# Padded routing matmuls, a static list of table loads and a new order of steps in a two-layer decoder kernel

## The chip, the cores and the metric

The kernel runs on one core of one Trainium2 chip. Its time is device microseconds; "before" is the median of 3 runs. The engines are PE (TensorE, with its weight loads as PEld), DVE (VectorE), ACT (ScalarE), POOL (GpSimd) and SP, which issues most DMAs.

## The reference

The input is x, 2 batches of 512 tokens with 128 features, fp32. Six sublayers follow one another, each as

```
x = layernorm(x + f(x))
```

with these f, in order:

1. a Hawk block: RMS norm, `z = xn @ W_in.T`, a causal convolution of 4 taps on one half, gates `sigmoid(xc @ W_gates.T + b)`, a linear recurrence `h = alpha*h + beta*inp*xc`, `gelu(gate)*h @ W_out.T`, and a gated MLP;
2. cross-attention with 8 heads to a context of 32 positions, masked;
3. causal attention with 16 heads from 32-wide latents with rotary parts, then 1 shared and 7 routed experts, the 2 best with weights `scores / sum(scores)`;
4. a selective state-space recurrence with 16 states per feature, `h = exp(delta*A)*h + delta*x*B`, `y = sum(h*C)`;
5. cross-attention with 4 heads that scales and shifts a diagonal state-space convolution (done as a discrete Fourier transform by matmuls), and an MLP of width 512;
6. two shared experts (together 352 wide, padded to 3 units of 128) and 8 routed experts of width 176 (11 units of 128), the 2 best.

Routing picks by rank; the weight of each routed expert is per token:

```
wts = sum(one_hot(idx, ER) * scores[..., None], axis=1)
combined = einsum('tei,eih,te->th', silu(g) * u, Wd_r, wts)
```

## The kernel before, in words

Features (or tokens, for scores and routing) lie on the 128 partitions, and an operation mostly handles a tile of 128 x 512, one batch's tokens. The batches are two lanes, a and b, each with a 16-slot workspace (`AR`), 4 of the 8 PSUM banks (`own(b, i)`) and its own list of steps per engine (`STEPS`). A third lane, w, holds work on weights alone (`STEPS_W`): folded projections of both cross-attentions, centred weights, the tables of the state-space kernel (`dt`, `z`, `a`, `dc` on 128 x 128 tiles, then `tP` to `Q` on POOL, `s1` to `eQ` on ACT, `r1.` to `P` on DVE, `kp` on PE), in two halves 0 and 1.

Each step is a piece of a Python generator that ends in `yield`: waits on semaphores of other steps (`after`), one or some instructions, and a count on its own semaphore (`done`). `take_turns` merges the three lanes of an engine into one in-order queue by the hand-held list `TURNS`: "a4 w1" is four steps of a, then one of w. An instruction behind a waiting one on its engine waits too. SP has an order of its own: loads, then a's drafts and stacks for attention (`parts(0)`), a wait for both batches' `xa.o`, two loads, `parts(1)`.

Steps that the prediction names, in a lane's order. Hawk block: `h1.sq`, norm, `z0` to `z3`, convolution (`cv` on ACT, `cw` on DVE), four gate steps `g0` to `g3` of two 128-deep fp32 matmuls each (two PE passes per matmul), tanh `tf`, `ti`, then `al`, `sa`, `lb`, `hb` on ACT, scans `h0`, `h1` on DVE, output matmul `rg` (line 553), norm `h4`, growth `gr`, `shr`, `ln1`, which ends in DVE's `X1`. Context attention: scores `xa.s` (line 581, with the mask row added by line 582), softmax on DVE and ACT, `xa.o` (line 596), `ln2`. Latents: `lat`, `kf`, `q0`, `q1`, `v` (line 621), the rotation on DVE, the split of keys and queries into three bf16 parts (a on DVE, b on POOL). Attention: for each of 8 pairs of heads five score tiles whose row maxima DVE takes (`mx0.A` to `mx7.E`); the maxima are split, transposed (`nmt`), copied by ACT into `wT` and sent by a DMA into the query stack; then 40 score units `su` with an Exp each, values `pv` and a normalisation. Experts (`units`): for unit k a gate matmul (line 729), an up matmul (line 734), from unit `shared` on a routing matmul (line 745), which spreads the token weights of one expert over 128 partitions, and a down matmul (line 756); ACT takes a tanh of the gate, DVE multiplies three times. The scan: for each of 16 states PE spreads B and C (`bn`, `cn`, lines 803 and 797, bf16, 96 rows), ACT makes the decay (`aa`) and a copy (`bb`), POOL a product (`by`), DVE a scan (`sc`, line 1659) and a product (`hc`), PE adds it up (`yn`, line 810). In `sel0` and `sel1` the rows behind the 21 or 24 used ones are zero.

In ACT's helper `f`, a change of activation function to one that the loaded table set lacks puts a table load in the queue, behind the waits of that step and in front of its activation.

Of the kernel before, what the change touches and what calls it, by code (L numbers as in the profile page):

```python
# [19 lines left out]
BF16 = mybir.dt.bfloat16  # L20
# [8 lines left out]
J = 32  # L29
# [23 lines left out]
KROWS = MROWS + 3  # L53

# [66 lines left out]
def _centre(t):  # L121
# [54 lines left out]
    "pool": ["va0", "va1", "e1", "fb.r", "fb.s", "fb.c", "bh", "bf", "bf1", "se0", "se1", "la", *[f"dc{i}" for i in range(1, 24)], "hd.c",  # L176
# [15 lines left out]
    "dve":  # L192
# [7 lines left out]
    "act":  # L200
# [6 lines left out]
    "pool":  # L207
        "w23 b1 w1 b5 w24 a2 w3 a3 w1 a4 b1 a1 b2 a2 b1 a1 b3 a3 b1 a1 b6 w1 b3",
}

# [46 lines left out]
def build(nc, dram, out):  # L257
    lay = layouts()
    with ExitStack() as ctx:
# [176 lines left out]
        def take_turns(engine, programs):  # L436

            for turn in TURNS[engine].split():
                for _ in range(int(turn[1:])):
                    next(programs[turn[0]])  # L440
            for program in programs.values():
                assert next(program, "end") == "end", engine
# [1824 lines left out]
```

## Time and profile before

| | |
|---|---|
| median of 3 runs | 563.76 us (562.29 to 564.13) |
| the profiled execution | 561.39 us |
| its span, first to last instruction | 559.6 us |
| PE busy | 471.7 us, 84% |
| DVE busy | 355.7 us, 64% |
| ACT busy | 294.1 us, 53% |
| POOL busy | 123.0 us, 22% |
| mean granted TensorE clock | 0.928 |

The profiled execution is 1.8 us longer than its span. All durations of the rows below belong to it. A share of busy time is a mean over stages; the chain of waits is followed back from the last instruction, at each step to what released it or to the instruction before it on its engine. An fp32 matmul shows as two records, one per pass.

### The profile page before, as it was taken

To read this page: it belongs to the slowest core of one execution; us is meant where nothing else is said; L and a number is where in the kernel's file an instruction comes from. 1 tells how busy PE (TensorE), PEld (TensorE's weight loads), DVE (VectorE), ACT (ScalarE), POOL (GpSimd) and SP (SyncE) were. 2 spreads that over 40 slices of the span, in tenths; PEclk is the share of its full clock that TensorE was granted. 3 is DMA by queue.
4 is the path that set the end of the run, shared out by engine and by line. 5 is a ranking of instruction groups with operands and counts; after the bars stand their busy time and mean duration, and the time that the engine had idled before them with its cause. 6 is when DMAs were issued, how large, how long until landed. Compare 5 with 4: busy or idle time off the path is not lost.

```text
span 559.6 us, 5894 instructions
## 1 busy us (share of the span) xinstructions
PE 471.7 (84%) x2098; PEld 210.6 (38%) x2098; DVE 355.7 (64%) x619; ACT 294.1 (53%) x447; POOL 123.0 (22%) x125
## 2 busy tenths in 40 slices
PE   5949867667859989998899758789899889999995
PEld 1523322332314544443343213337646334343331
DVE  1485835546875854556888899886452264676764
ACT  4736784514104657788559866475145274542123
POOL 2000300000630008108454977334000000000000
PEclk9968796957887999999999979989999999999999
DMA  8920000633360000033000000060000000000001
GB/s 311 273 112 1 1 0 0 182 45 129 116 112 3 0 5 2 1 152 150 1 2 0 1 0 0 11 234 1 0 1 0 0 1 0 0 1 1 0 1 38
DMA packets 8983, 26.38 MB, mean 47 GB/s; under 512 B 2959, under 2 KB 6768, under 8 KB 7664
## 3 DMA queue, kind: packets, MB, share of 16 engines
q1 hardware_dynamic: 8852, 25.91, 14.8%
q8 instruction: 16, 0.26, 0.2%
q10 hardware_dynamic: 102, 0.10, 0.1%
q14 instruction: 13, 0.11, 0.1%
HBM read 21.98 MB, written 3.67 MB: 46 GB/s over the span
## 4 chain that ended last, share of the span: by engine, by line
PE 56%; DVE 17%; ACT 11%; POOL 6%; issue 5%; DMA 3%; SPq 1%; DVEq 0%; ACTq 0%
ACT AR L1012 7%; PE PS L756 5%; PE PS L729 5%; DVE AR L1339 5%; PE PS L734 5%; PE PS L818 4%; DVE stats L1348 4%; PE PS L659 3%; ACT L1011 3%; POOL RR L2024 3%; PE PS L673 3%; PE PS L527 3%; POOL AR L1936 3%; PE PS L547 2%; DMA AR<-in_s4d 2%
## 5 line engine op out<-in xcount | busy, mean ns | idle before, releaser
L1012 ACT ACTIVATE AR<-PS 128x512 f32<-128x512 f32 (+1 forms) x198 | 111.6, 594 | 118.3 <-PE PS L729 59.8
L1936 POOL TENSOR_TENSOR AR<-AR 128x512 f32<-128x512 f32 (+2 forms) x48 | 53.4, 1128 | 96.1 <-DVE AR L1339 74.4
L1012 ACT ACTIVATE AR<-AR 128x512 f32<-128x512 f32 (+2 forms) x72 | 43.8, 618 | 55.8 <-DVE AR L1339 38.0
L1011 ACT ACT_TABLE_LOAD x38 | 48.8, 1283 | 23.5 <-PE PS L527 6.1
L1339 DVE TENSOR_TENSOR AR<-PS,AR 128x512 f32<-128x512 f32 x74 | 50.3, 686 | 11.8 <-PE PS L797 3.6
L1348 DVE TENSOR_REDUCE stats<-PS 128x1 f32<-128x512 f32 (+4 forms) x88 | 43.4, 524 | 19.1 <-PE PS L645 7.6
L1345 DVE SCALAR_TENSOR_TENSOR AR<-AR,PS 128x512 f32<-128x512 f32 x44 | 29.8, 683 | 25.0 <-ACT AR L1012 24.7
L1659 DVE TENSOR_TENSOR_SCAN AR<-PS,AR 128x512 f32<-128x512 f32 x32 | 38.5, 1215 | 6.1 <-POOL AR L1936 4.3
L2024 POOL TENSOR_TENSOR RR<-KL,lags 128x512 f32<-128x512 f32 x24 | 28.2, 1211 | 62.3 <-PE PS L662 52.1
L642 PE MATMUL PS<-RR 97*128 97x512 bf16 (+3 forms) x128 | 32.6, 325 | 7.3 <-DVE stats L1348 3.6
L527 PE MATMUL PS<-AR,W_sq 128*128 128x512 f32 x44 | 25.9, 673 | 13.9 <-ACT AR L1012 13.8
L1345 DVE SCALAR_TENSOR_TENSOR AR<-PS,AR 128x512 f32<-128x512 f32 x44 | 30.1, 688 | 8.9 <-PE PS L745 4.8
L810 PE MATMUL PS<-AR,W_sq 128*128 128x512 f32 x64 | 34.3, 626 | 1.5 <-issue 1.5
L659 PE MATMUL PS<-RR 100*128 100x512 bf16 (+3 forms) x128 | 30.5, 313 | 3.8 <-DMA RR<-wT 2.2
L756 PE MATMUL PS<-AR,RR 128*128 128x512 f32 x56 | 30.8, 633 | 0.0
L729 PE MATMUL PS<-x_in,RR 128*128 128x512 f32 x56 | 28.6, 598 | 1.5 <-DVE AR L1345 1.5
L734 PE MATMUL PS<-x_in,RR 128*128 128x512 f32 x56 | 28.8, 596 | 0.0
L1012 ACT ACTIVATE AR<-PS,W_vec 128x512 f32<-128x512 f32 (+1 forms) x32 | 21.9, 696 | 12.4 <-PE PS L527 4.2
L1339 DVE TENSOR_TENSOR AR<-AR 128x512 f32<-128x512 f32 (+4 forms) x36 | 22.4, 640 | 5.8 <-ACT AR L1012 5.3
L1012 ACT ACTIVATE PS<-AR,W_vec 128x512 f32<-128x512 f32 x32 | 21.8, 689 | 7.7 <-DVE AR L1659 7.6
L797 PE MATMUL PS<-AR,select 96*128 96x512 bf16 x32 | 13.1, 415 | 10.8 <-DVE AR L1339 10.7
L673 PE MATMUL PS<-AR,Vaug 128*9 128x512 f32 (+3 forms) x256 | 21.8, 434 | 0.0
(231 smaller groups left out, 790.6 us busy)
## 6 DMA issues: line engine op xcount, KB each, us to landing
RR<-in_dft SPq DMA_DIRECT2D x1, 4096.0 KB, 12.1
RR<-in_ffn SPq DMA_DIRECT2D x1, 2688.0 KB, 9.6
RR<-in_ones SPq DMA_DIRECT2D x2, 832.0 KB
RR<-in_ones SPq DMA_DIRECT2D x2, 784.0 KB
RA<-in_moe SPq DMA_DIRECT2D x1, 1539.5 KB, 6.3
W_mla<-in_mla SPq DMA_DIRECT2D x1, 1504.0 KB, 16.8
W_late<-in_late SPq DMA_DIRECT2D x1, 1076.0 KB, 10.9
RA<-in_xa SPq DMA_DIRECT2D x1, 1056.0 KB, 8.6
```

The lines of the kernel that those rows point to most:

```text
L527: mm(own(b, i), w("sq", "ones"), A(b, 1), start=True, stop=True).then_inc(*done("pe", b, f"{t}.{step}"))
L659: mm(ring[:, c:c + n_], Kst[b][0:KROWS, h, 128 * kb:128 * kb + 128], Qst[b][0:KROWS, h, 128 * kb:T], start=(c == 0), stop=False)
L729: mm(own(b, 0), w(group, "g", 128 * k, 128), x, start=True, stop=True)\
L734: mm(own(b, 1), w(group, "u", 128 * k, 128), x, start=True, stop=True)\
L756: mm(own(b, 3), w(group, "d", 128 * j, 128), A(b, 6 + j % 2), start=(j == 0 and base is None), stop=(k == n))\
L1011: nc.scalar.preload_act_table_set(tables[loaded[0]])
L1012: nc.scalar.activation(out_, in_, func, bias=bias, scale=scale).then_inc(*done("act", *step))
L1339: nc.vector.tensor_tensor(out_, a, b_, op).then_inc(*done("dve", *step))
L1345: nc.vector.scalar_tensor_tensor(out_, a, s1, b_, op0, op1).then_inc(*done("dve", *step))
L1348: nc.vector.tensor_reduce(out_, a, X, op).then_inc(*done("dve", *step))
L1936: nc.gpsimd.tensor_tensor(out_, a, b_, op).then_inc(*done("pool", *step))
L2024: last = nc.gpsimd.tensor_tensor(out_[:, q:q + n], a[:, q:q + n], b_[:, q:q + n], op)
```

## The change

Three edits.

1. `wT` gets 96 rows instead of 48, `krowb` 96 instead of 1. Both are zeroed by POOL (steps `kz`, `wz0`, `wz1`), and the routing matmuls (line 745) and the mask-row matmuls (lines 582 and 833) read 96 rows. DVE's first write of `krowb` waits for `kz`, ACT's first write of `wT` for `wz`.
2. ACT's table loads stand in a static list `TABLES`, by place in the queue: `take_turns` calls `load_tables(n)` ahead of step n, and so ahead of its waits. The list has 30 entries.
3. `TURNS` is new for all four engines. In it b's steps of the Hawk block follow a's at a shorter distance on PE, DVE and ACT; on PE all of b's latents stand in front of a's first maximum; b's experts and b's scan come later relative to a's scan; POOL splits b's keys and queries ahead of `dc1` to `dc23`. DVE's Hawk block also waits for the load of `vec`. Of the long lists the first two lines stand below.

```diff
--- before.py
+++ after.py
@@ -51,6 +51,7 @@
 ZROWS = 49
 MROWS = PRODUCTS * HD + ZROWS
 KROWS = MROWS + 3
+WROWS = 96
 
 
 def _ln(t):
@@ -173,7 +174,7 @@
             *_centre("w2"), "hd.s", "hd.m",
             *[f"{n}{h}" for h in HALVES for n in ("r1.", "q1.", "r2.", "q2.", "rQ0.", "qQ0.", "rQ1.", "qQ1.", "P")],
             "ed.s", "ed.m"],
-    "pool": ["va0", "va1", "e1", "fb.r", "fb.s", "fb.c", "bh", "bf", "bf1", "se0", "se1", "la", *[f"dc{i}" for i in range(1, 24)], "hd.c",
+    "pool": ["kz", "va0", "va1", "e1", "fb.r", "fb.s", "fb.c", "bh", "bf", "bf1", "se0", "se1", "wz0", "wz1", "la", *[f"dc{i}" for i in range(1, 24)], "hd.c",
              *[f"{n}{h}" for h in HALVES for n in ("tP", "tQ", "aP", "aQ", "U1", "U2", "V", "Q")], "ed.c"],
 }
 
@@ -181,32 +182,39 @@
 
 TURNS = {
     "pe":
-        "a4 w1 a5 w3 a1 w1 a1 w2 a2 b1 a3 b2 a1 b2 a2 b3 a1 b1 a3 b1 a1 b1 a3 b4 a1 b7 a2 b1 a9 b4 a1 b1 a29 b1 "
-        "a2 b1 a1 b1 a2 b1 a1 b2 a2 b1 a1 b1 a1 b2 a1 b1 a3 b3 a3 b2 a1 b1 a2 b2 a3 b2 a1 b1 a2 b1 a1 b1 a1 b2 "
...
+        "a4 w1 a5 w6 a1 b1 a1 b2 a1 b2 a1 b4 a4 b1 a2 b4 a1 b1 a1 b1 a1 b1 a1 b2 a3 b2 a2 b7 a36 b1 a1 b1 a3 b3 "
+        "a1 b5 a2 b1 a1 b1 a1 b1 a1 b1 a2 b2 a1 b1 a1 b1 a1 b2 a1 b1 a1 b1 a2 b1 a1 b1 a2 b3 a2 b1 a2 b2 a1 b2 "
...
     "dve":
-        "a7 w2 a1 w3 a1 w6 a1 w1 a4 w1 a1 w3 a2 w1 a1 w6 a1 w2 a1 w3 b1 w3 b1 w2 b1 w1 b2 a1 b2 a1 w2 a6 w2 a3 "
-        "b1 a1 b5 a1 b2 a1 b2 a1 b1 a5 b2 a4 b12 a4 b1 a5 b1 w1 a1 b1 w1 b3 a34 b16 a1 b7 a1 b7 a2 b14 a1 w1 a3 "
...
+        "a2 w4 a5 w1 a2 w6 a1 w1 a1 w5 a1 w1 a3 w8 a1 w1 a1 w4 b1 w1 a1 w1 b7 a1 b1 w5 a1 b6 a1 b1 a2 b1 a2 b1 "
+        "a6 b2 a2 b2 a1 b9 a8 b1 a2 b6 a36 b1 a4 b2 a4 b9 w1 b1 w1 b12 a1 b8 a1 b6 a1 b1 a1 b4 a5 w1 b1 a1 b1 "
...
     "act":
-        "a1 w2 a2 w1 a3 w1 a1 w1 b1 w1 a17 b2 w1 b1 a1 b1 a2 b2 w2 a1 b2 a1 b3 a1 b2 a1 b3 a1 b2 a7 b2 a1 b3 a5 "
-        "b20 a1 b1 a37 b1 a4 b2 a1 b1 a1 b2 a1 b6 a1 b4 a1 b10 a1 b2 a1 b1 a1 b2 a1 b2 a1 b5 a1 b3 a1 b3 a1 b1 "
...
+        "a4 b1 w2 a3 w1 a1 w2 a1 w1 a10 b1 a1 b1 a2 b2 a1 b1 w1 a1 b1 w1 b3 w1 b9 a3 b1 a1 b2 a1 b2 a2 b1 a1 b1 "
+        "a1 b1 a6 b1 a1 b3 a4 b1 a1 b13 a31 b1 a8 b1 a1 b1 a1 b1 a1 b1 a1 b1 a2 b6 a1 b5 a1 b3 a2 b1 a1 b1 a1 "
...
     "pool":
-        "w23 b1 w1 b5 w24 a2 w3 a3 w1 a4 b1 a1 b2 a2 b1 a1 b3 a3 b1 a1 b6 w1 b3",
+        "w14 b1 w1 b5 w35 a4 w1 a3 w3 a6 w1 a4 b12 w1 b5",
 }
+
+
+
+TABLES = (
+    "1:log 8:gelu 10:log 11:exp 22:log 33:gelu 38:sin 44:log 60:gelu 62:log 182:exp 195:sin 199:exp "
+    "211:log 215:exp 219:log 221:exp 226:log 227:exp 240:sin 246:exp 263:log 346:gelu 350:log 361:gelu "
+    "370:log 373:exp 376:log 378:exp 402:log")
 
 
 def steps_of(engine, lane):
@@ -347,7 +355,7 @@
                                     sb("tmask", [128, B * NT // 4], U32))
         kmask, krow, tmask = (m[:, :].bitcast(U8) for m in (kmask_w, krow_w, tmask_w))
         tmaskf = sb("tmaskf", [128, B * NT])
-        krowb = sb("krowb", [1, B * (H0 + H1) * J], BF16)
+        krowb = sb("krowb", [WROWS, B * (H0 + H1) * J], BF16)
         pre = flat(0, 11, 14)
         kmaskf, KTs, VTs, K1s, Vrep = (pre[:, 0:512], pre[:, 512:768], pre[:, 768:1024], pre[:, 1024:1088],
                                        pre[:, 1088:1344])
@@ -364,7 +372,7 @@
         stats = sb("stats", [128, B * 1024])
         parts48 = sb("parts", [128, B, NT, 48], BF16)
         spb = [parts48[:, b] for b in range(B)]
-        wT = [sb(f"wT{b}", [48, T], BF16) for b in range(B)]
+        wT = [sb(f"wT{b}", [WROWS, T], BF16) for b in range(B)]
         Vaug = [sb(f"Vaug{b}", [128, NT, NH, HD + 1]) for b in range(B)]
         KL = sb("KL", [128, NT, 128])
         Kf = sb("Kf", [128, 2, NFB, 128])
@@ -433,11 +441,12 @@
         block = ctx.enter_context(nc.Block())
 
 
-        def take_turns(engine, programs):
-
-            for turn in TURNS[engine].split():
-                for _ in range(int(turn[1:])):
-                    next(programs[turn[0]])
+        def take_turns(engine, programs, before=lambda n: None):
+
+            lanes_ = [turn[0] for turn in TURNS[engine].split() for _ in range(int(turn[1:]))]
+            for n, lane in enumerate(lanes_):
+                before(n)
+                next(programs[lane])
             for program in programs.values():
                 assert next(program, "end") == "end", engine
 
@@ -579,7 +588,7 @@
                     for i in range(2):
                         c = own(b, p)[:, 256 * i:256 * i + 256]
                         mm(c, Xin[b][:, 128 * (2 * p + i):128 * (2 * p + i) + 128], M0[:, b, :], start=True, stop=False)
-                        last = mm(c, w("bf", "one")[0:1, :], krowb[:, 256 * b:256 * b + 256], start=False, stop=True)
+                        last = mm(c, w("bf", "one")[0:WROWS, :], krowb[:, 256 * b:256 * b + 256], start=False, stop=True)
                     last.then_inc(*done("pe", b, f"xa.s{p}"))
                     yield
                 for p in range(2):
@@ -742,7 +751,7 @@
                         elif k > shared:
                             pe.wait_ge(*after("dve", b, f"{d}w{k - 1}"))
                         if k >= shared:
-                            mm(own(b, 2), w(sel, "s", 128 * (k - shared), 128)[0:3 * e, :], wT[b][0:3 * e, :],
+                            mm(own(b, 2), w(sel, "s", 128 * (k - shared), 128)[0:WROWS, :], wT[b][:, :],
                                start=True, stop=True).then_inc(*done("pe", b, f"{p}w{k}"))
                             yield
                     if k:
@@ -830,7 +839,7 @@
                 for i in range(NT):
                     c = own(b, 2)[:, 128 * i:128 * i + 128]
                     mm(c, Xin[b][:, 128 * i:128 * i + 128], M1[:, b, :], start=True, stop=False)
-                    last = mm(c, w("bf", "one")[0:1, :], krowb[:, 512 + 128 * b:640 + 128 * b], start=False, stop=True)
+                    last = mm(c, w("bf", "one")[0:WROWS, :], krowb[:, 512 + 128 * b:640 + 128 * b], start=False, stop=True)
                 last.then_inc(*done("pe", b, "xb.s"))
                 yield
                 pe.wait_ge(*after("dve", b, "xb.p"))
@@ -1004,11 +1013,15 @@
                       "sin": "silu_and_others"}
             in_all = (ACT.Square, ACT.Copy, ACT.Identity, ACT.Abs)
             loaded = ["none"]
+            at_step = dict(x.split(":") for x in TABLES.split())
+
+            def load_tables(n):
+                if str(n) in at_step:
+                    loaded[0] = at_step[str(n)]
+                    nc.scalar.preload_act_table_set(tables[loaded[0]])
 
             def f(out_, in_, func, step, bias=0.0, scale=1.0):
-                if func not in in_all and func not in sets.get(loaded[0], ()):
-                    loaded[0] = "log" if func == ACT.Exp else next(k for k, v in sets.items() if func in v)
-                    nc.scalar.preload_act_table_set(tables[loaded[0]])
+                assert func in in_all or func in sets[loaded[0]], (step, func, loaded)
                 nc.scalar.activation(out_, in_, func, bias=bias, scale=scale).then_inc(*done("act", *step))
 
             def root(b, t, i):
@@ -1133,10 +1146,11 @@
                     act.wait_ge(*after("act", "w", "sy"))
                     act.wait_ge(*after("dve", "w", "a6"))
                     act.wait_ge(*after("pool", "w", "dc23"))
+                act.wait_ge(*after("pool", "w", f"wz{b}"))
                 act.wait_ge(*after("pe", b, "nmt"))
                 f(wT[b][0:48, :], own(b, 0).bitcast(BF16)[0:48, 0:T], ACT.Copy, (b, "nmt"))
                 act.wait_ge(*after("act", b, "nmt"))
-                act.dma_start(Qst[b][MROWS:KROWS, :, :], wT[b][:, :]).then_inc(stack["m", b], 16)
+                act.dma_start(Qst[b][MROWS:KROWS, :, :], wT[b][0:48, :]).then_inc(stack["m", b], 16)
                 yield
                 for n in range(GROUPS * UNITS + LAG):
                     if n < GROUPS * UNITS:
@@ -1330,7 +1344,7 @@
                 f(KL[:, :, :].rearrange("p j d -> p (j d)"), own(0, 0), ACT.Copy, ("w", "kl"))
                 yield
 
-            take_turns("act", {"a": batch(0), "b": batch(1), "w": shared_program()})
+            take_turns("act", {"a": batch(0), "b": batch(1), "w": shared_program()}, load_tables)
 
 
         @block.vector
@@ -1361,6 +1375,7 @@
                 tt(Xin[b][:, :], src, A(b, 7), ALU.mult, (b, name))
 
             def hawk(b):
+                dve.wait_ge(loads["vec"], 16)
                 dve.wait_ge(*after("act", b, "h1.r"))
                 stt(A(b, 2), Xin[b][:, :], vec("g1"), A(b, 7), ALU.mult, ALU.mult, (b, "xn1"))
                 yield
@@ -1790,10 +1805,11 @@
                     dve.wait_ge(loads[n], 16)
                 copy(kmaskf, kmask, ("w", "km"))
                 yield
-                copy(krowb[:, :], krow, ("w", "kb0"))
+                dve.wait_ge(*after("pool", "w", "kz"))
+                copy(krowb[0:1, :], krow, ("w", "kb0"))
                 yield
                 mine("w", "kb0")
-                ts(krowb[:, :], krowb[:, :], -1.0, BIG, ALU.add, ALU.mult, ("w", "kb1"))
+                ts(krowb[0:1, :], krowb[0:1, :], -1.0, BIG, ALU.add, ALU.mult, ("w", "kb1"))
                 yield
                 copy(tmaskf[:, :], tmask, ("w", "tm"))
                 yield
@@ -1974,6 +1990,8 @@
                     yield
 
             def shared_program():
+                nc.gpsimd.memset(krowb[:, :], 0.0).then_inc(*done("pool", "w", "kz"))
+                yield
                 for b in range(B):
                     nc.gpsimd.memset(Vaug[b][:, :, :, :], 1.0).then_inc(*done("pool", "w", f"va{b}"))
                     yield
@@ -2004,6 +2022,9 @@
                 mine("w", "se0")
                 tt(select[0:96, :], select[0:96, :], third[2], ALU.add, ("w", "se1"))
                 yield
+                for b in range(B):
+                    nc.gpsimd.memset(wT[b][:, :], 0.0).then_inc(*done("pool", "w", f"wz{b}"))
+                    yield
 
                 def quarters(table, l):
                     return table.rearrange("p (q i) l -> p q i l", q=4)
```

## Rows read from the trace of the kernel before

**Rows 1.** Stages: length, busy us (instructions) by engine, PE clock, DMA share, GB/s.
```profile
42.00:126.00 84.00, 63.44 (x139) 25.44 (x138) 45.44 (x79) 47.76 (x69) 5.97 (x11) 0.78 0.17 38
126.00:165.00 39.00, 30.36 (x132) 11.46 (x130) 31.57 (x69) 8.38 (x13) 14.22 (x19) 0.85 0.48 128
165.00:180.00 15.00, 11.26 (x73) 5.89 (x74) 6.82 (x15) 7.10 (x12) 0.00 (x0) 0.68 0.01 3
180.00:300.00 120.00, 111.62 (x808) 50.02 (x800) 82.82 (x160) 84.40 (x133) 40.24 (x34) 1.00 0.09 37
300.00:400.00 100.00, 82.63 (x440) 42.02 (x440) 80.77 (x97) 61.36 (x97) 58.67 (x45) 0.95 0.10 34
400.00:560.00 160.00, 145.60 (x403) 62.15 (x402) 87.96 (x159) 62.94 (x91) 0.00 (x0) 0.99 0.01 4
```

**Rows 2.** The chain that ended last, pieces: start us, us, what.
```profile
36.08 3.80 PE PS L553 x4
...
59.45 0.70 DVE x_in L1339
...
87.02 3.78 PE PS L553 x4
...
101.79 1.08 PE PS L621 x8
...
123.46 3.70 PE PS L596 x4
...
153.43 1.39 DVE stats L1348 x3
...
156.55 1.39 DVE stats L1348 x3
...
165.89 3.75 DMA RR<-wT
...
552.54 1.28 ACT L1011
```

**Rows 3.** PE's timeline, a unit of the tail and rows of the scan: start, us.
```profile
534.48 1.02 PE L734 MATMUL PS<-x_in,RR 128*128 128x512 f32 x2
535.44 0.39 PE L745 MATMUL PS<-wT,RR 24*128 24x512 bf16 x1
535.75 1.13 PE L756 MATMUL PS<-AR,RR 128*128 128x512 f32 x2
536.72 1.02 PE L729 MATMUL PS<-x_in,RR 128*128 128x512 f32 x2
...
341.05 0.38 PE L797 MATMUL PS<-AR,select 96*128 96x512 bf16 x1
341.26 1.02 PE L810 MATMUL PS<-AR,W_sq 128*128 128x512 f32 x2
342.12 0.38 PE L803 MATMUL PS<-AR,select 96*128 96x512 bf16 x1
```

**Rows 4.** Loads of x (SP issue, DMA landing) and POOL's first memsets.
```profile
L447 SPq DMA_DIRECT2D x_in<-in_x x2: 377/936/1494, 0.7 to 4.7; - x2
...
DMA to landing us min/median/max: 3.2/6.5/9.8
...
0.71 1.10 POOL L1978 MEMSET Vaug<- 128x576 f32 x2 [0.29 <-POOLq L2260]
```

**Rows 5.** The page's group of table loads: count, busy, mean ns, idle before.
```profile
L1011 ACT ACT_TABLE_LOAD x38 | 48.8, 1283 | 23.5 <-PE PS L527 6.1
```

**Rows 6.** ACT's timeline around the load for `dt`: start, us, idle before.
```profile
18.10 1.28 ACT L1011 ACT_TABLE_LOAD   x1 [1.75 <-DMA AR<-in_s4d]
19.39 0.31 ACT L1012 ACTIVATE AR<-AR 128x128 f32<-128x128 f32 x1
```

**Rows 7.** DVE's groups of 297 to 400 us: count, busy, mean ns, idle before.
```profile
L1659 DVE TENSOR_TENSOR_SCAN AR<-PS,AR 128x512 f32<-128x512 f32 x32 | 38.5, 1215 | 6.1 <-POOL AR L1936 4.3 <-ACT PS L1012 1.4
L1339 DVE TENSOR_TENSOR AR<-PS,AR 128x512 f32<-128x512 f32 x36 | 24.2, 683 | 4.5 <-PE PS L797 3.6
```

30 rows, old and new, of the table TURNS are left out of this document.

## The prediction

> **What bounds the kernel now.** I read the busy time by stage first, then the chain that ended last, then single rows. I call the two batches a and b; b runs about 42 us behind a. The stages [rows 1] show three regimes. Up to 126 us (Hawk block, context attention, latents of both batches) no engine is full: in 42 to 126 TensorE is busy 63.4 us of 84 although its granted clock is only 0.78, that is, it moves between 1.2 and 2.4 GHz, ACT 47.8 and DVE 45.4. This stretch is bound by latency: PE, ACT and DVE hand one 0.6 to 0.9 us operation to each other. From 126 to 165 the row maxima of batch a bound it, on DVE. From 180 on TensorE is the bound: 111.6 of 120 us, and 145.6 of 160 us from 400. Between them, 300 to 400, PE has 17.4 us idle; there DVE, with 80.8 us, carries the two recurrences (32 scans of 1.2 us [rows 7]).
>
> The chain of waits [rows 2] gives marks that I use below: a's `rg` ends at 39.9, a's `X1` is at 59.5, b's `rg` at 87.0, a's values at 101.8, b's context output matmul at 123.5 to 127.2, the maxima at 3.12 us per pair of heads, and the 3.75 us DMA of a's row maxima into the query stack at 165.9.
>
> **Part 1, padding the small matmuls to 96 rows.** The edit makes 36 routing matmuls (14 in the first expert layer, 22 in the second) and 8 mask-row matmuls read 96 rows instead of 21, 24 or 1. What it changes is read from start to start [rows 3]. In an expert of the tail: up projection at 534.48, routing matmul (24 rows) at 535.44, down projection 535.75, next gate projection 536.72, so 0.96, 0.31 and 0.97. In the scan, where the same sort of matmul has 96 rows between the same 128-row fp32 pairs: 341.05, 341.26, 342.12, so 0.21 and 0.86. The 24-row matmul thus costs 0.10 in front, 0.10 behind and 0.11 in the pair after it: 0.31 us per unit, 3.09 to 2.78. The dependent loop of a unit (two passes of the gate matmul, a tanh and a multiply of 0.6 to 0.7 us each) stays under that, and DVE's 88 and ACT's 63 us of 160 [rows 1] say that neither engine is full. So 22 x 0.31 = 6.8 us in the second layer, where PE is full; in the first, 14 x 0.31 = 4.3, of which at least three fall after 300, where PE has gaps. Bounds 0 (if the difference comes from elsewhere) and 44 x 0.31 = 13.6; I take 8.
>
> One rule speaks against this part. The Trainium skill (TensorE: Matmul & The Clock Gate, Step-by-step: what each phase is for) says that a weight load's time goes with its columns, and the row count doesn't matter. The load rows agree in themselves (0.09 to 0.10 us either way), but the start distances don't. By the rule alone the 8 us would be 0.
>
> What is added: three memsets on POOL (`kz`, `wz0`, `wz1`, 768 and twice 512 columns). By the 576-column one, 0.55 us each [rows 4], they take 0.5 to 0.8 us. `kz` is waited for by DVE's mask copy alone, which waits for a DMA issued about when b's x is; ACT's wait on `wz` comes 100 us after. Uncovered they would cost 1.8 us, covered 0.
>
> **Part 2, table sets in front of the waits.** Before, 38 loads of 1.283 us, 48.8 us [rows 5], each issued after the wait of its activation; 30 remain. The chain holds 14 of them, 17.9 us (the last is the row at 552.54 in [rows 2]). Where ACT was idle before the activation for 1.28 us or more, a load in front of the wait is free; where ACT is packed it still costs. Most of the front's 16 loads are in the walk below, so I count only the rest here: from 180 on the chain holds 8, most of them while PE, the bound, has other work. PE's idle in 440 to 560 is small, so 3 us; bounds 0 and 8 x 1.28 = 10.3.
>
> A load at 18.10 is followed by its activation at 19.39 [rows 6]: 1.28 us, nothing behind it. The Trainium skill (ScalarE: Activation LUTs, What ACT_TABLE_LOAD costs) puts a switch at about 2.66 us, with a drain of 1.38; the row contradicts it. By the page, this part would be worth about twice as much, 6 us.
>
> **Part 3, the order.** Each engine is one in-order queue; the lists decide what stands in front of what. I walk the new lists with the old durations.
>
> *Start.* ACT's copy of b (`h1.sq`) now stands in front of a's second conv step. b's x lands at 4.7 + 9.8 = 14.5 [rows 4], so a loses about 2.6 us; DVE's mask steps, which wait for DMAs issued just before it, lie under that. The table for `lb` is now its own load (+1.3), `fb.l` and `dt` no longer hold up tanh (before, ACT stood until 18.1 for the DMA of `dt` [rows 6]), and DVE does the shared `m1` before a's scans. Sum: a's `rg` ends at about 44 instead of 39.9.
>
> *Hawk block.* b's first norm follows at once, in front of a's next step. b's four gate steps stand in front of a's last growth steps, and ACT does b's whole gate chain before a's `ln1`. b: norm to conv 10.5, four gates 6.9 at full clock (16 passes of 0.43), tanh to square root 8, two scans and products 5, so b's `rg` at about 74 instead of 87.0. a's `X1` falls behind, to about 74 instead of 59.5.
>
> *Until the maxima.* a then takes 42 us less b's gates (7.4) and some waits: a's values at about 107, against 102. b is level with it: context output at about 108 instead of 123.5, and 16 us of norm, latents and rotation later its values at 124. PE now takes all of b's latents before a's first maximum, which starts at 124 (before: 127, behind b's context output in the queue; no DMA stands in the chain there [rows 2]).
>
> *Maxima.* Before, b's latents split the first three pairs, and the maxima's DMA came at 165.9. Now DVE has only the eight pairs, 8 x 3.12 = 25 us, and behind them the old 3 us of small steps (splits, transposes, a copy): the DMA comes at 124 + 25 + 3 = 152. This is the largest term; for the walk's roundings I count 13 of the 14 us. Its bounds: 0 if a's lateness is not made up, 22 if the clock rises with the denser order (63.4 us of PE work at mean clock 0.78).
>
> *Attention.* b's first maxima now fill the DMA wait of a (3.75 us, PE had next to nothing), and b's maxima are transposed seven score units earlier, which covers the second such DMA. PE idles 3.7 of 15 us there at clock 0.68; with some of the second wait I take 5 us, bounds 0 and 8.
>
> *Scan stage.* Before, the rows of a and b alternate from 327 to 360; now a's scan has b's experts beside it and b's scan a's state space. POOL (58.7 us busy) still does its table steps U1, U2, V and Q1 between a's rows, which stalls a's scan as before. DVE has 80.8 us of work in these 100 us, one row alone costs DVE 1.9 us (scan 1.22, product 0.68 [rows 7]). PE's idle 17.4 us is what can be won; I take 5, between a loss of 10 and a gain of 17, nearer to what DVE's 19 us of idle allow once POOL's stalls remain.
>
> **Sum.** 13 + 5 + 8 + 3 + 5 = 34 us. The profiled execution took 561.4 us (span 559.6, 1.8 us around it), 2.4 below the median 563.8. 561.4 - 34 = 527.4, beside the median 529.8: I say 530.
>
> **The rivals.**
> - *The order gives nothing in the end* (20%). The maxima end earlier, but PE, full from 180, meets the lost time again in a scan stage that now runs its recurrences one after the other, with POOL's tables between rows. For it: DVE is at 81% there, and b's scan starts some twenty steps later relative to a's. Left: padding 8, loads 3, and 5 of the waits, 563.8 - 16 = 548.
> - *The scan stage gives back its idle time too* (14%). Two alternating scans stall each other's in-order queues; apart they don't. 12 of the 17.4 us more than none, and the front gains 5 to 10 more by the clock: 530 - 7 - 9 = about 514.
> - *Padding does nothing* (7%), the rule above: 530 + 8 = 538.
> - *Slower* (9%): b's gate matmuls in front of a's steps at the lower clock. The same PE work of 42 to 126 wholly at 1.2 GHz is 63.4 x 0.78 / 0.5 = 99 us, 15 more than the stretch has, and a's 13 us lateness at `X1` then stays. +28, less 21 for the other parts: 561.4 + 7 + 2.4 = about 571. It decides if the front loses more than 21 us, that is, if the DMA of a's maxima comes later than about 187. Against it: a's mark at 127 has slack behind a queue, and a denser queue should raise the clock rather than lower it.
>
> My own case has 50%. A measurement of this kernel can't tell 0.3% (1.7 us) from no change. Faster takes my case and the first three rivals but a piece of the first and of my own lower bounds: 0.86. Same 0.05, slower 0.09. The range leaves out the slower case and the end of the large one: 511 to 555. My case alone: 519 to 541.
>
> **What would show it.** In the changed profile: 30 table loads with the idle time ahead of them hardly ended by anything but the previous activation; routing matmuls of 96 rows 0.21 us ahead of the down projection and a tail period near 2.78 us; b's `rg` near 74 and a's `X1` near 74; DVE without a gap over all eight pairs of a's maxima, their DMA near 152; no PE stop behind the DMA of the maxima; b's recurrence beginning when a's ends, with the last row near 365 to 380. Wrong, if the tail period stays 3.09 (padding), if that DMA comes after 165 (order of the front), or if PE's idle time in the scan stage grows beyond 17 us.

## The result, and the profile after

The changed kernel takes 538.97 us (median of 4 runs, 537.76 to 542.13), the one before on the same chip 563.94 us (562.29 to 564.61): ratio 0.957, 95% interval 0.952 to 0.962, some 25 us. I had said 530, with 511 to 555. The profiled execution took 538.7 us, its span is 536.9.

The stages of the changed kernel, cut as in [rows 1] (length, busy us and instructions of PE, PE weight loads, DVE, ACT, POOL, granted clock, DMA share, GB/s):

```profile
42.00:126.00 84.00, 63.30 (x152) 26.07 (x151) 46.99 (x82) 46.97 (x73) 0.00 (x0) 0.83 0.18 41
126.00:165.00 39.00, 31.39 (x154) 14.12 (x152) 34.89 (x79) 4.73 (x8) 17.73 (x30) 0.75 0.47 123
165.00:180.00 15.00, 15.00 (x120) 8.37 (x122) 11.77 (x26) 8.20 (x15) 1.90 (x1) 0.86 0.01 1
180.00:300.00 120.00, 108.77 (x745) 48.79 (x738) 79.61 (x149) 89.50 (x139) 50.64 (x44) 0.99 0.09 36
300.00:400.00 100.00, 84.05 (x455) 43.90 (x454) 79.68 (x99) 58.76 (x94) 47.24 (x36) 0.97 0.10 35
400.00:537.00 137.00, 126.79 (x371) 58.88 (x369) 78.23 (x144) 54.28 (x80) 0.00 (x0) 0.99 0.01 4
```

In 165 to 180 PE has no gap left (it had 3.7 us), but the window no longer holds the same work: a's DMA of the maxima, which made that gap, now lies ahead of it. In 300 to 400 PE still idles 16 us (17.4 before). That window too is shifted: the first scan starts at 286.1 (308.8 before), the last at 381.2 (392.3). So the scans begin 23 us earlier and end 11 us earlier; from the first to the last of them PE idles 14.6 us where it idled 16.9 (286 to 382 against 308.8 to 393.5).

The chain around the front's marks, in order of time (start us, us, what); it answers to [rows 2]:

```profile
71.72 2.96 PE PS L562 x4
...
106.37 1.06 PE PS L625 x2
...
119.77 1.94 PE PS L614 x2
121.71 2.01 PE PS L616 x2
123.72 1.53 PE PS L617 x2
125.24 0.62 PE PS L619
...
126.40 1.30 DVE AR L1353 x2
...
127.74 1.55 PE PS L630 x8
129.30 0.54 PE PS L651
...
129.98 0.69 DVE stats L1362
...
156.12 0.80 DVE stats L1362 x2
...
159.15 3.76 DMA RR<-wT
```

L562 is b's `rg`, L614 to L630 are b's latents up to its values, L651 is the first score matmul for a's maxima. The DMA of the maxima comes at 159.15, where it was 165.89; I had it at 152. PE still waits for it, in front of the first score unit (idle time in brackets):

```profile
162.96 0.61 PE L668 MATMUL PS<-RR 100*128 100x512 bf16 x1 [1.42 <-DMA RR<-wT]
```

Before, PE stood 2.76 us for ACT at this place and then 0.98 for the DMA.

A unit of the tail on PE, against [rows 3]: 0.22 and 0.86 us where 0.31 and 0.97 stood, the period 2.80 instead of 3.09.

```profile
517.83 0.38 PE L754 MATMUL PS<-wT,RR 96*128 96x512 bf16 x1
518.05 1.02 PE L765 MATMUL PS<-AR,RR 128*128 128x512 f32 x2
518.91 1.02 PE L738 MATMUL PS<-x_in,RR 128*128 128x512 f32 x2
519.77 1.02 PE L743 MATMUL PS<-x_in,RR 128*128 128x512 f32 x2
520.63 0.38 PE L754 MATMUL PS<-wT,RR 96*128 96x512 bf16 x1
```

The table loads and the scans (busy, mean ns, idle before), against [rows 5] and [rows 7]. The loads no longer stand behind waits: 0.5 us of idle ahead of 30, against 23.5 ahead of 38.

```profile
L1021 ACT ACT_TABLE_LOAD x30 | 38.5, 1283 | 0.5
...
L1674 DVE TENSOR_TENSOR_SCAN AR<-PS,AR 128x512 f32<-128x512 f32 x32 | 38.9, 1217 | 8.6 <-ACT PS L1025 5.8
```

To see where time was won I laid the two traces over each other by the share of all matmul columns streamed so far. The changed kernel reaches the same share 13 us earlier at 120 (time of the kernel before), 9 at 160 and 200, 9.5 at 280, 12 at 320 to 400, 14 at 440, 19 at 520, 21 at 540. I call this the overlay below; it compares single executions, and two executions of the changed kernel (this one and that of x0 below) lie 3 us apart in it. So 9 us come from the front and the maxima, 3 from the first expert layer and the scans, and the rest of the span's 22.7, some 10, from the tail.

### The profile page after: what moved, and what is told of

Its sections match the earlier page's. It is cut to its first block, busy times and chain, and to the rows that moved or that the text cites. A ratio compares the mean times of both kernels' runs of the same rounds, so it can differ in the third digit from the quotient of the medians.

```text
span 536.9 us, 5892 instructions
## 1 busy us (share of the span) xinstructions
PE 456.7 (85%) x2098; PEld 214.3 (40%) x2098; DVE 351.5 (65%) x619; ACT 284.0 (53%) x439; POOL 122.3 (23%) x128
## 4 chain that ended last, share of the span: by engine, by line
PE 59%; DVE 21%; ACT 9%; issue 4%; DMA 3%; SPq 2%; DVEq 0%; ACTq 0%
ACT AR L1025 6%; PE PS L738 6%; PE PS L765 6%; PE PS L743 5%; DVE AR L1353 5%; DVE stats L1362 4%; PE PS L827 4%; DVE AR L1359 4%; PE PS L668 3%; PE PS L556 3%; PE PS L682 3%; PE PS L877 3%; PE PS L819 2%; DVE AR L1674 2%; PE PS L536 2%
## 5 line engine op out<-in xcount | busy, mean ns | idle before, releaser
L1952 POOL TENSOR_TENSOR AR<-AR 128x512 f32<-128x512 f32 (+2 forms) x48 | 52.1, 1092 | 136.7 <-DVE AR L1353 107.5
L1025 ACT ACTIVATE AR<-AR 128x512 f32<-128x512 f32 (+1 forms) x72 | 43.8, 617 | 37.2 <-DVE AR L1353 19.2
L651 PE MATMUL PS<-RR 97*128 97x512 bf16 (+3 forms) x128 | 35.5, 355 | 5.0 <-DVE stats L1362 3.8
L536 PE MATMUL PS<-AR,W_sq 128*128 128x512 f32 x44 | 25.6, 665 | 13.1 <-ACT AR L1025 12.9
L765 PE MATMUL PS<-AR,RR 128*128 128x512 f32 x56 | 28.6, 594 | 0.2 <-DVE AR L1359 0.2
L654 PE MATMUL PS<-W_bf 128*128 128x256 bf16 (+1 forms) x80 | 23.3, 291 | 0.0
```

Source lines behind the costliest of these rows:

```text
L765: mm(own(b, 3), w(group, "d", 128 * j, 128), A(b, 6 + j % 2), start=(j == 0 and base is None), stop=(k == n))\
L1025: nc.scalar.activation(out_, in_, func, bias=bias, scale=scale).then_inc(*done("act", *step))
L1952: nc.gpsimd.tensor_tensor(out_, a, b_, op).then_inc(*done("pool", *step))
```

## The experiments

The change has three parts: padding (P), table loads in front of the waits (L), the new order (O). I ran all their combinations, then split the padding and the order. "Before" was timed beside each of them, so a row is read by its ratio; the intervals are some 0.5 to 1 point either way. POOL's memsets and DVE's wait for `vec` stay in all of them.

| kernel | median us | ratio to before | 95% interval |
|---|---|---|---|
| P alone (x1) | 552.45 | 0.984 | 0.974 to 0.995 |
| L alone, 38 loads (x2) | 560.04 | 0.998 | 0.993 to 1.002 |
| O alone, 33 loads (x3) | 565.70 | 1.010 | 1.001 to 1.019 |
| O and L (x4) | 555.42 | 0.989 | 0.980 to 0.998 |
| O and P (x5) | 550.99 | 0.982 | 0.976 to 0.987 |
| P and L, old order (x6) | 544.99 | 0.970 | 0.965 to 0.975 |
| all three, once more (x0) | 539.8 | 0.959 | 0.954 to 0.963 |
| all, mask rows unpadded (x7) | 547.66 | 0.977 | 0.971 to 0.982 |
| new order up to the maxima (x10) | 549.0 | 0.978 | 0.974 to 0.981 |
| new order from the maxima on (x11) | 544.36 | 0.967 | 0.963 to 0.971 |

The changed kernel once more, in five rounds, as the measure for all the others:

> The changed kernel itself, again, on one chip with the next three. Theory 1: ratio 0.957 as before. If the earlier 0.957 owed some us to where the clock happened to fall, it comes out at 0.965 to 0.97.

**Padding alone.**
```
 TURNS: as before; loads: behind the waits as before
-w(sel, "s", ...)[0:3 * e, :], wT[b][0:3 * e, :]
+w(sel, "s", ...)[0:WROWS, :], wT[b][:, :]
 (and krowb from 1 to 96 rows)
```


> Before with the padding alone (96-row routing and mask matmuls, their memsets), old order, table loads behind the waits. Theory 1, padding acts by itself where PE is full: 22 units of the second layer lose 0.30 us each (6.6 us) and the first layer's 14 and the 8 mask rows another 1 to 3 us: 8 to 9 us faster than before, ratio about 0.985, tail period 2.80 us. Rival, the old order's waits absorb it: under 3 us, though the tail period is 2.80.

1.6% or some 9 us, near the 8 of my sum, with an interval of 3 to 15 us; the tail period is 2.80.

**Loads alone.** The 38 loads of the old list, each put in front of its wait.
```
-loads in f(), behind act.wait_ge
+take_turns("act", ..., load_tables)   # same 38 loads, by step number
```


> Before with its 38 table loads in front of the waits, same places, old order, no padding. Idle time of ACT ahead of the loads, up to 1.28 us each, sums to 14.8 us over the kernel. Theory 1: about half of it lies on the chain (the loads of 18 to 107 us and those at 427 and 441): 5 to 7 us faster. Rival: PE's cold clock and b's slack take it up: under 2 us. Upper bound 14.8.

0.2%, within the interval nothing, though the idle time in front of the loads went from 23.5 to 0.7 us. In the overlay x2 leads by 3 us at 120 and still by 2.5 at 320, and has lost it all by 360. This trace is of the slowest of x2's ten executions (563.2 us, median 560.0), so the loss may be that execution's more than the kernel's. Two stages of it, then the same of before:

```profile
320.00:340.00 20.00, 13.80 (x29) 4.95 (x30) 17.10 (x22) 11.84 (x20) 12.57 (x11) 0.74 0.00 0
...
360.00:380.00 20.00, 15.97 (x48) 7.02 (x49) 16.07 (x21) 13.28 (x23) 6.71 (x5) 0.86 0.48 169
```
```profile
320.00:340.00 20.00, 12.43 (x32) 4.17 (x31) 17.66 (x23) 12.40 (x22) 14.46 (x12) 0.83 0.00 0
...
360.00:380.00 20.00, 17.37 (x53) 7.99 (x54) 17.66 (x24) 15.03 (x26) 6.71 (x5) 0.91 0.48 169
```

The granted clock is lower in both (0.74 for 0.83, 0.86 for 0.91). The loss goes with the clock; what brought either about I did not separate.

**Order alone**, and with the loads.
```
+TURNS = { the new lists }
 [0:3 * e, :] and krowb[0:1, ...] as before; loads behind the waits (33 in this order)
```


> Before with the new order alone: no padding, loads behind the waits (the rule then makes 33). Theory 1, the order is worth about 10 us by the maxima of a that run without b's latents in between: ratio 0.982. Rival, the order was only good with the loads hoisted, because it packs ACT with both batches' Hawk blocks: no gain or slower.

```
+TURNS = { the new lists }, TABLES = { the new list }
 [0:3 * e, :] and krowb[0:1, ...] as before
```


> After without the padding (21, 24 and 1 rows read, memsets kept). Theory 1: 8 to 9 us slower than after, so ratio to before about 0.972, and the tail period 3.09 us. Rival, the padding matters less than its 36 x 0.30 us: 4 us or less slower than after.

The order by itself makes the kernel slower, by 1.0% (0.1 to 1.9). In the overlay x3 leads the kernel before by 8 us at 160 to 240, by 3 at 360, by nothing at 420, and is 3 behind at 520. The front keeps its promise, and it is given back behind 240. With the loads in front (x4) a lead of 4 to 8 us holds to 440. But x4 misses what I expected of it: 0.989 is 17 us behind the changed kernel, not 8 to 9.

**Order and padding, loads behind the waits.**
```
-"w": shared_program()}, load_tables)
+"w": shared_program()})               # and the load again in f(), behind the wait
```


> After with the table loads behind the waits again (33 by the old rule instead of 30). The order alone was 1.0% slower than before, the order with hoisted loads 1.1% faster. Theory 1: the new order packs ACT, so it needs the loads in front of the waits: 10 to 12 us slower than after, lost in the scan stage (240 to 400 us) and not in the front. Rival: the loads cost their 1.28 us at places where PE waits for them, 3 to 5 us in all.

Its loads (first row) against those of the kernel before [rows 5]:

```profile
L1026 ACT ACT_TABLE_LOAD x33 | 42.3, 1283 | 18.6 <-PE PS L536 8.9 <-PE PS L890 5.5 <-PE PS L569 1.3
```

Up to 240 x5 runs within 2 us of the full change (x0's trace, the fastest of its six executions); it then falls 4 us behind at 300, 8 at 360, 12 at 480. By the medians it is 11 us, as my first theory had it, though part of it falls behind 400. Half of the idle time in front of its loads is ended by L536, the mean-square matmul of a norm: PE sums, ACT loads log, ACT answers, DVE scales. My reading, which no run tests by itself, is that PE has little else at these points and that a load behind the wait is on the path there.

**Padding and loads in the old order.**
```
 TURNS: as before
+[0:WROWS, :], krowb[:, ...], and 38 loads in front of the waits
```


> Before with padding and hoisted loads, old order. Alone they gave 8.7 and 1.3 us. Theory 1, they add up: 10 us faster than before, ratio 0.982. Then the order, on top of both, is worth the rest of after's gain, some 14 us, though alone it lost 6. Rival: each removes a wait that covered the other: 14 us or more already.

0.970: the two small parts alone bring 3.0%, and the order another 1.1 points of the 4.1. With this run all eight combinations are there, and each part can be priced in the company of the others (points of the time before, positive is faster):

| part | alone | with one other | with both |
|---|---|---|---|
| P | 1.6 | 2.8 (L), 2.8 (O) | 3.0 |
| L | 0.2 | 1.4 (P), 2.1 (O) | 2.3 |
| O | -1.0 | 0.2 (P), 0.9 (L) | 1.1 |

The order gains little more than a point at best, and clearly so only beside both others; the three parts alone sum to 0.8 points, together they make 4.1, and that difference is clear of the intervals. That L is worth more with P than without it is not.

Where x6's gain comes from shows in part in its front:

```profile
42.00:126.00 84.00, 61.64 (x169) 25.30 (x167) 55.12 (x97) 52.53 (x76) 6.31 (x11) 0.86 0.22 59
126.00:165.00 39.00, 30.38 (x131) 12.67 (x135) 25.55 (x58) 7.83 (x13) 14.21 (x19) 0.73 0.38 83
165.00:180.00 15.00, 15.00 (x145) 8.33 (x138) 11.44 (x27) 8.42 (x15) 0.00 (x0) 1.00 0.00 1
```
```profile
L1151 ACTq DMA_DIRECT2D RR<-wT x2: 760/1054/1347, 154.6 to 195.7; - x2
```

In 42 to 126 the clock is 0.86 (before 0.78 [rows 1]) and the DMAs of the two batches' maxima are issued at 154.6 and 195.7 (the row of ACT's queue: ns min/median/max, first and last start). The changed kernel's:

```profile
L1153 ACTq DMA_DIRECT2D RR<-wT x2: 742/1045/1348, 159.2 to 193.7; - x2
```

So the old order, padded and with early loads, has a's maxima done no later than the new order (159.2 here, 155.7 in x0), and b's 2 to 5 us later. In the overlay x6 leads x1 by 7 us at 120, more than L alone gave there (3). The clock goes with it: from 20 to 180 us it stood at 1.2 GHz for 51 us in x6 and for 68 in before and in x1. It need not be the whole cause: the two executions of the changed kernel stood there 64 and 51 us, and differ by 3 us in the overlay.

**The mask rows.**
```
-w("bf", "one")[0:WROWS, :], krowb[:, ...]
+w("bf", "one")[0:1, :], krowb[0:1, ...]      # both mask-row matmuls, all else as changed
```


> After with the 8 mask-row matmuls on 1 row again; the 36 routing matmuls stay on 96. In the kernel without any padding the front was 3.6 us later by 120 us. Theory 1: the mask rows cost 0.1 to 0.2 us each and at most 2 us in all. Rival: they are behind those 3.6 us, and this kernel is 3 to 4 us slower than after.

I had expected 2 us at most, or 3 to 4 by the rival; it costs 7.9 us of median, 10 by the ratios (0.977 against 0.959). PE in a's state space, first x7 and then the changed kernel (start, us):

```profile
350.54 0.49 PE L841 MATMUL PS<-M,x_in 128*128 128x128 f32 x2 [2.04 <-DVE x_in L1353]
350.96 0.22 PE L842 MATMUL PS<-krowb,W_bf 1*128 1x128 bf16 x1
351.12 0.49 PE L841 MATMUL PS<-M,x_in 128*128 128x128 f32 x2
351.54 0.23 PE L842 MATMUL PS<-krowb,W_bf 1*128 1x128 bf16 x1
```
```profile
347.74 0.22 PE L842 MATMUL PS<-krowb,W_bf 96*128 96x128 bf16 x1
347.80 0.44 PE L841 MATMUL PS<-M,x_in 128*128 128x128 f32 x2
348.08 0.22 PE L842 MATMUL PS<-krowb,W_bf 96*128 96x128 bf16 x1
```

The mask matmul's own duration is the same, and the fp32 pair is recorded only 0.05 us longer; the distances tell: 0.58 us from one mask matmul to the next against 0.34. In context attention I read 0.84 against 0.55 at 2.4 GHz and 1.47 against 1.07 at 1.2. With 4, 4 and 8 of each that is 4 x 0.29 + 4 x 0.40 + 8 x 0.24 = 4.7 us. The rest, 3 us by the medians and 5 by the ratios, I did not separate. In 350 to 370 x7 was granted a lower clock than x0 (x7, then x0):

```profile
350.00:360.00 10.00, 9.28 (x24) 4.05 (x24) 8.64 (x11) 5.71 (x11) 2.54 (x2) 0.66 0.00 1
360.00:370.00 10.00, 8.20 (x20) 3.82 (x20) 7.57 (x10) 4.47 (x9) 2.54 (x2) 0.83 0.00 1
```
```profile
350.00:360.00 10.00, 8.73 (x22) 3.60 (x23) 8.93 (x11) 5.80 (x11) 2.68 (x3) 0.83 0.00 1
360.00:370.00 10.00, 9.28 (x57) 6.32 (x56) 6.83 (x10) 6.31 (x12) 7.30 (x4) 1.00 0.01 2
```

Against x4, x7 gives the price of the routing rows alone: 555.42 - 547.66 = 7.8 us, or 1.2 points by the ratios, 7 us. The two were timed at different times, and their intervals leave some 6 us either way.

**How many rows are enough.** The 36 routing matmuls on 64 and on 32 rows.
```
-w(sel, "s", ...)[0:WROWS, :], wT[b][:, :]
+w(sel, "s", ...)[0:64, :], wT[b][0:64, :]        # or 0:32
```


> The changed kernel with the 36 routing matmuls on 64 rows instead of 96. Theory A (TensorE pays for a change of the row group, and 64 rows is another group than 128): up to routing to down projection 0.31 us and more, tail period 3.09 instead of 2.80, end some 8 us later, 547. Theory B (only a count below a full 32 rows, or below 32, pays): 0.22 and 2.80 as with 96 rows, 539.

> The same with 32 rows. Theory A: tail period 3.09, 547 us. Theory B: 2.80, 539 us. If 64 is free and 32 is not, the line lies between them: 2.80 in the run on 64 rows and 3.09 here.

The tail on 64 rows:

```profile
527.70 1.02 PE L743 MATMUL PS<-x_in,RR 128*128 128x512 f32 x2
528.65 0.39 PE L754 MATMUL PS<-wT,RR 64*128 64x512 bf16 x1
528.97 1.12 PE L765 MATMUL PS<-AR,RR 128*128 128x512 f32 x2
529.93 1.02 PE L738 MATMUL PS<-x_in,RR 128*128 128x512 f32 x2
```

0.95, 0.32, 0.96: period 3.09, to the hundredth what 24 rows cost [rows 3], and 32 rows give the same. The single times are 544.1 us (64 rows) and 551.5 (32); with the same period they differ by 7 us, beside mean granted clocks of 0.942 and 0.920, so the whole time says little here. Theory A held on the period: 1, 24, 32 and 64 rows pay, 96 don't. The Trainium skill (TensorEngine Tiling (Array Packing), Tiling Modes) says that a change of the tiling mode drains TensorE, and lists modes of 32, 64 and 128 rows; these distances fit it, with 96 rows as part of the full array. No run shows a drain as such. The row-count rule of the Trainium skill that I weighed in the prediction (TensorE: Matmul & The Clock Gate, Step-by-step: what each phase is for) holds for a load's own duration (0.09 to 0.10 us) and says nothing of the distance.

**The order, cut in two** at the end of a's maxima, with P and L in both.
```
 x10: per engine, steps of the new list up to 156.8 us, the rest in the old list's sequence (30 loads)
 x11: steps of the old list up to 163.4 us, the rest in the new list's sequence (35 loads)
```


> Padding and loads in front of the waits as in the changed kernel (30 loads); each engine follows the new list up to the end of a's maxima and the old list from there on. Read so far: with the old list, padding and early loads alone bring the DMA of a's maxima to 154.6 us, no later than the new list does (155.7 and 159.2). Theory (the order's gain lies behind the maxima): that DMA again at 155 to 160, the end like the old order with both other parts, 545 us, ratio 0.970. Rival (it lies in the front, by b's earlier arrival): 539 us, ratio 0.958. Rival (the two halves fit only each other): over 550, ratio above 0.98.

> The reverse: the old list up to the end of a's maxima, the new list from there on, padding and loads in front of the waits (35 loads). Theory (gain behind the maxima): DMA of a's maxima at 154 to 156, and from there the new list's pace, so 536 to 539 us, ratio 0.955 or a little less, the best of all. Rival (gain in the front): 545 us, ratio 0.970. Rival (the new rest needs b as early as the new front makes it; b's stacks and values come some 10 us later here): over 550 us.

x10 is worse than the old order throughout (549.0 against 545.0), x11 no better than it by the medians (544.4, 0.967 against 0.970). By the timed runs neither half has the gain of the whole (0.959). My theory said 536 to 539 us for x11 and is not borne out; the rival (front) falls with x10; the third, that the halves need each other, is nearest, but its numbers (over 550 for both) were not reached either. The DMA of a's maxima came at 160.1 in x10, and in x11 at 159.1, not at 154 to 156.

x10's loss has a place, the seam. There PE stands ahead of the transposes and again for a's DMA; x10, then the same DMA in before:

```profile
158.71 0.62 PE L704 MATMUL PS<-W_bf,parts 128*48 128x128 bf16 x4 [3.85 <-DVE parts L1352]
163.86 0.61 PE L667 MATMUL PS<-RR 100*128 100x512 bf16 x1 [4.53 <-DMA RR<-wT]
```
```profile
169.69 0.61 PE L659 MATMUL PS<-RR 100*128 100x512 bf16 x1 [0.98 <-DMA RR<-wT]
```

Nothing of b stands at this place in x10's queue: b's latents are done, and b's first score matmuls, which the new list puts there, come later in the old list. At b's own DMA x10 waits no longer than before (1.22 and 1.25 us).

The traces show something that the medians hide. Laid over x6, the changed kernel, x0 and x11 are behind by 2 to 5 us at 280 and ahead by 5 to 8 at 420: some 10 us are won between these marks by all three kernels that have the new list there. x10, which has the old one, wins 4. The clock accounts for some of it: from 280 to 420 it stood at 1.2 GHz for 14 us in x6 and for 7 in each of the other four. What is left between x10 and the three, some 6 us, goes with the new list. So the place of the order's gain, beside P and L, is the scan stage; how much of it stays in the total is for the timed runs to say, and there x11 kept next to nothing (its trace, 540.2 us, is the fastest of its six).

## Why the prediction came out as it did

The number was 9 us too low and the range held, but by luck: two errors offset each other. I had given the order's terms 23 of the 34 us (13, 5 and 5) and the other two parts 11. On top of the other two, the order measured 5 to 6, and the other two by themselves 17. The step that failed is the largest term, 13 us, with the 5 of the waits: that the order brings a's maxima forward and that this is carried to the end. Alone it does bring them forward, but x3 gives it back behind 240; beside P and L it brings nothing up to 280, where the changed kernel is 2 to 5 us behind x6, and what the order gives then comes from the scan stage.

- **The marks of the front** up to 108 were right (87.0, which I gave for b's `rg` before, is its start; it ended at 90.8, so the gain there is 16 us): a's `rg` 43.9 (44 said), b's 74.7 (74), a's `X1` 72.7 (74), a's values' matmul at 106.9 (107), b's context output 108.0 (108).
- **"16 us of norm, latents and rotation later its values at 124" failed.** They came at 127.7 to 129.3, and a's first maximum at 129.2, not 124. Of the 5 us, 1.4 stand between b's context output and its residual, where DVE does a's last splits first (`s2` at 111.4); most of the rest is the low clock: six passes of L614 to L617 take 5.5 us in the chain above, and six at 0.43 us, as at 2.4 GHz, are 2.6. I had used full-clock durations in a stretch in which PE had just stood idle for 5.8 us (114.0 to 119.8; granted clock 0.50 from 116 to 122). And "no DMA stands in the chain" was true only for before. There the DMAs of a's stacks land at 119.7, 7 us ahead of their use. In the changed kernel the last piece is issued at 116.3 and lands at 127.3, so 124 was out of reach in this execution whatever b's latents did.
- **Maxima, 13 us said:** the DMA came 6.7 us earlier in the profiled execution (10 in x0's). DVE took 26.9 us for the eight pairs and b's first units between them, not 25. And beside P and L none of it is the order's: alone it brings that DMA to 159.9 (x3), but P and L in the old order bring it to 154.6 (x6), and all three together no further. I had put onto the order what padding, early loads and the clock that follows them bring too.
- **Waits of the maxima, 5 said:** "no PE stop behind the DMA" did not come true. The gap of 165 to 180 is gone because the DMA now lies ahead of that window; PE stands 1.4 us at it (3.7 before, most of it for ACT) and 0.3 at the second (1.25 before). That is 3 us less idle time, at a granted clock of 0.50 around the first DMA, and the overlay shows no gain from 160 to 200.
- **Padding, 8 said:** the routing term was right as far as the runs tell (7 to 8 us, x4 against x7; period 2.80, where I had 2.78). The mask rows were mis-sized: I counted 8 matmuls and gave them nearly nothing. There are 16, at 0.24 to 0.40 us, 4.7 us by the distances and 8 to 10 by the timed runs. P is worth 9 us alone and about 16 with L (0.998 to 0.970) or with O (1.010 to 0.982).
- **Loads behind 180, 3 said (0 to 10.3):** x5 against x0 is 11 us, nearly all behind 240. That is at my upper bound, within what the two intervals leave, and far from the 3. The term priced only the 8 loads that the chain of before held there; that more of them are on the path once other waits are gone is my reading of x5's rows, not separated. Alone, in the old kernel, all 38 were worth 1 us.
- **Scan stage, 5 said:** PE's idle time fell from 17.4 to 16 us, the last scan starts at 381.2 (392.3 before; 365 to 380 said) against 384.1 in x6. That is 3 us. Measured from 280 to 420 against x6, it is 10 in the traces, of which some 6 are the list's (above): this is where the order pays, and I had given it the smaller share.
- **Rivals.** "The order gives nothing in the end" was close to the mechanism: on top of P and L it gives 5 to 6 us (0.970 to 0.959), with neither it costs 6, with P alone it gives nothing. Its 548 missed because P and L give 17, not 11. "Padding does nothing" and "slower" fell. For 514 the clock would have had to rise further: the mean granted clock is 0.928 in both profiled executions.

What is not settled: why L gives nothing in the old kernel and 11 to 13 us in the new one beyond what the clock's stretches show, and why x11, which has the new list in the scan stage, keeps so little of it by its median.

## What to carry to other kernels

Price the parts of a change in each other's company: here three parts worth -1.6, -0.2 and +1.0% alone made -4.1% together, and an order that gains with the loads in front lost without them. My reading is that what one part frees another uses. Read the cost of small matmuls from start to start, not from durations, and count them in the trace; if one must stand between full-height matmuls, fill its rows to 96. Where PE has been idle, walk the next steps with durations from a stretch at 1.2 GHz (six passes took 5.5 us there, where I had reckoned with 2.6).

## What I had not expected of the hardware

- Between 128-row matmuls, one of 1, 24, 32 or 64 rows lengthens the sequence by about 0.3 us at 2.4 GHz (0.24 to 0.29 read, against 96 rows), and one of 1 row by 0.40 at 1.2. Its own record hardly shows it (0.39 us on 24 and 64 rows, 0.38 on 96); the matmul pair behind it is recorded up to 0.1 us longer (1.12 to 1.13 against 1.02), and the rest shows only from start to start.
- The time at 1.2 GHz differs much between orders and even between executions of one kernel: from 20 us on, 81 us in before, 89 in x1, 72 in x6, 77 and 64 in two executions of the changed kernel, whose spans were 536.9 and 533.5. Six timed runs of that kernel spread over 535.3 to 544.3.
- A table load takes 1.283 us wherever it stands; what its place is worth depends on what else waits. Put in front of the waits, the idle time ahead of 38 loads went from 23.5 to 0.7 us, and the kernel gained 0.2%; in the new order with padding the same move gained 2.3 points.
